# A two-layer transformer tower on one core: unread matmuls in front of TensorE's waits, attention's later stages one half step back, and three steps moved

## The reference

```python
h = tok_ffn(x[..., 0])                       # relu(x W0^T) * (x W1^T), times Wo^T
h = layernorm(h + window_attention(h))       # 16 heads of 16, |i - j| <= 64
h = layernorm(h + bitlinear_ffn(h))          # activations rounded to 8 bits, weights to -1, 0, 1
h = layernorm(h + causal_attention(h))
h = layernorm(h + moe(h))                    # 8 experts, top 2, at most 640 rows each
```

## Time and profile before

| | |
|---|---|
| time, 3 runs | 1106.05 us median, 1106.0 to 1106.23 |
| the profiled execution | 1107.4 us, its span 1105.7 us |
| PE busy | 880.9 us (80%), 4838 matmuls |
| PE weight load busy | 550.9 us (50%) |
| DVE busy | 542.7 us (49%) |
| ACT busy | 418.2 us (38%) |
| POOL busy | 297.8 us (27%) |
| mean granted TensorE clock | 0.899 of full speed |
| DMA | 81.48 MB |

### The profile page before, as it was taken

How to read it: one execution, slowest core, us unless ns; L and a number is a source line. 1 busy time by engine, 2 the same in 40 slices (tenths; PEclk the granted TensorE clock), 3 DMA queues, 4 the chain that set the end, 5 groups by cost and what they waited for, 6 DMA issues and landing times. The chain is left out here.

```text
span 1105.7 us, 14051 instructions
## 1 busy us (share of the span) xinstructions
PE 880.9 (80%) x4838; PEld 550.9 (50%) x4838; DVE 542.7 (49%) x2103; ACT 418.2 (38%) x717; POOL 297.8 (27%) x364
## 2 busy tenths in 40 slices
PE   6697889768688778888968788633999999999940
PEld 3454445534444434434524434321677787778830
DVE  1267424768668678777785777241021112111137
ACT  1325324466466476576545445300312211221002
POOL 5002312413413413212333242415021122112232
PEclk9897999979979889988988979665999999999975
DMA  9873250631532523412365420106113441343242
GB/s 355 134 179 42 30 65 15 67 37 22 61 36 35 61 24 44 54 21 27 45 90 73 56 62 21 40 24 259 56 20 115 124 128 22 113 124 66 24 100 76
DMA packets 57446, 81.48 MB, mean 74 GB/s; under 512 B 6560, under 2 KB 50977, under 8 KB 54944
## 3 DMA queue, kind: packets, MB, share of 16 engines
q1 hardware_dynamic: 49456, 70.48, 31.9%
q0 software_dynamic: 7296, 9.47, 5.1%
q10 hardware_dynamic: 624, 0.63, 0.2%
HBM read 35.37 MB, written 19.68 MB: 50 GB/s over the span
## 5 line engine op out<-in xcount | busy, mean ns | idle before, releaser
L1031 DVE CUSTOM_DVE_ANT_0 junk<-ps,maskb 128x256 bf16<-128x256 f32 (+4 forms) x512 | 205.9, 435 | 118.3 <-PE ps L755 117.1
L583 ACT ACTIVATE probs<-ps 128x512 f32<-128x512 f32 (+1 forms) x304 | 158.0, 550 | 103.0 <-PE ps L778 100.4
L1498 PE MATMUL ps<-dxT,w1s 128*128 128x320 f32 x512 | 141.9, 439 | 2.3 <-DVE dxT L1562 2.3
L1510 PE MATMUL ps<-w2s,hTe 128*128 128x256 f32 x640 | 139.3, 379 | 0.0
L1510 PEld LDWEIGHTS ps<-w2s,hTe 128*128 128x128 f32 x640 | 121.1, 190 | 16.3
L1532 ACT ACTIVATE hTe<-ps,b1s 128x640 f32<-128x640 f32 x64 | 50.8, 794 | 204.6 <-PE ps L1498 204.6
L1457 POOL DMA_INDIRECT mixed_rows<-ysb,ids x40 | 61.7, 1543 | 228.9 <-DVE ysb L1580 226.0
L755 PE MATMUL ps<-ks,qs 96*128 96x256 bf16 (+4 forms) x512 | 107.4, 294 | 19.9 <-DMA ks<-parts 8.7
L778 PE MATMUL ps<-qs,ks 99*128 99x256 bf16 (+4 forms) x512 | 107.3, 297 | 19.1 <-DMA qs<-nrows 7.9
L1498 PEld LDWEIGHTS ps<-dxT,w1s 128*128 128x128 f32 x512 | 98.5, 193 | 43.7 <-DVE dxT L1562 2.9
L794 PE MATMUL ps<-probs,vaug 128*32 128x256 f32 (+4 forms) x1024 | 94.9, 447 | 13.6 <-POOL probs L493 12.4
(11 more groups left out here) (171 smaller groups left out, 1196.3 us busy)
## 6 DMA issues: line engine op xcount, KB each, us to landing
qs<-parts SPq DMA_DIRECT2D x96, 128.0 KB, 4.9
ks<-parts SPq DMA_DIRECT2D x96, 128.0 KB, 7.5
w1s<-w SPq DMA_DIRECT2D x8, 1024.0 KB, 9.4
w2s<-w SPq DMA_DIRECT2D x8, 1024.0 KB, 4.9
dispatched_rows<-att SPq DMA_DIRECT2D x8, 650.0 KB, 16.5
dx<-dispatched_rows SPq DMA_DIRECT2D x8, 650.0 KB, 7.6
x_sb<-xT SPq DMA_DIRECT2D x8, 256.0 KB, 6.1
mixed_rows<-h SPq DMA_DIRECT2D x4, 512.0 KB, 5.6
```

What stands on the lines that cost most here:

```text
L583: act.activation(probs_of(u)[:, heads[0]:heads[-1] + 1, :], turned_bank((u, half, i))[:, 0:len(heads) * w].rearrange("p (j n) -> p j n", n=w),
L1031: ins = dve.tensor_tensor_reduce(out=junk[:, AT["s", (u, half, i)][0], a * (hi - lo):(a + 1) * (hi - lo)], in0=score_bank((u, half, i))[:, ...
L1498: ins = mm(bank(2 * (n % 2) + c)[:, 0:HC], w1s[:, e % 2, k, m * P:(m + 1) * P], dxT[:, e % 2, k, c * HC:(c + 1) * HC], start=(k == 0), sto ...
L1510: ins = mm(bank(4 + n % 2)[:, 0:D], hTe[:, e % 2, m, t * P:(t + 1) * P], w2s[:, e % 2, m, :], start=(m == 0), stop=(m == MH - 1))
```

## The change

A helper issues matmuls whose result nobody reads: `identb` (128x128) times 512 columns of `maskb`, both bf16, into the PSUM bank that is opened next and overwritten by the real work.

It is called with the bank already open and ahead of the wait: 24 times before the first scores (unit 0, whose wait for the first stack moves behind them), 12 before each of the four `fqT` turns, 3 before each of the 16 `f` turns, 10 before the turn of `gate` 3 only, 10 before each of the four counts `cnt`, 12 before `wq` 0 only, and 8 (written out) in the experts' block. Its core, with the other edits:

```diff
-TO_ROWS, TO_TURNED, TO_VALUES, TO_BACK, TO_HEADS = 10, 14, 18, 27, 28
+TO_ROWS, TO_TURNED, TO_VALUES, TO_BACK, TO_HEADS = 11, 15, 19, 28, 29
-STEPS = {... "route": 12 ...}
+STEPS = {... "route": 13 ...}
 # SP
+def load_x(b):
+    sp.wait_ge(*d_full(("tok", b - 1, f"u{ME - 1}")))
+    for k in range(KD):
+        sp.dma_start(x_sb[:, k, :], xT[0, k * P:(k + 1) * P, b * S:(b + 1) * S]).then_inc(x_in, 16)
-if phase == "tok" and c == 8 and i + 1 < B:
...
+if phase == "tok" and c == 8 and i < 2:
+    load_x(i + 1)
+if phase == "qkv" and i == 1 and c == 5:
+    load_x(3)
 if phase == "qkv":
     for j, part in STACKS[c]:
 # POOL
-if phase == "qkv" and c == 7:
+if phase == "qkv" and c in (6, 7):
...
-    for k in range(2):
+    for k in (c - 6,):
...
-if phase == "route" and c >= 8:
-    t = c - 8
+if phase == "route" and c >= 9:
+    t = c - 9
 # ACT
-if (eta - 25) % 8 == 0 and 0 <= eta - 25 < 2 * UNITS:
+if (eta - 26) % 8 == 0 and 0 <= eta - 26 < 2 * UNITS:
 # PE
 if phase == "ffn" and c == FQT:
+    o = d_open(("ffn", i, "fqT"))
+    keep_busy(o, 12)
+    o = o.bitcast(BF16)
     pe.wait_ge(fq_done, i + 1)
...
-if phase == "route" and c == 3:
+if phase == "route" and c == 5:
+    o = d_open(("route", i, "cnt"))
+    keep_busy(o, 10)
     pe.wait_ge(chosen, i + 1)
 # DVE, in route(i, c): the steps that follow the count
-if c == 5:
+if c == 6:
-if c == 6:
+if c == 7:
-if c == 7:
+if c == 8:
 # experts' block, SP
 def load_rows(e):
+    if e:
         sp.dma_start(dx[:, e % 2, :, :], dx_v[e]).then_inc(rows_in[e % 2], 16)
+    else:
+        for t in range(CT):
+            sp.dma_start(dx[:, 0, t, :], dx_v[0][:, t, :]).then_inc(first_in[t], 16)
 # experts' block, PE
 def turn_rows(e):
-    pe.wait_ge(rows_in[e % 2], 16 * (e // 2 + 1))
+    if e:
+        pe.wait_ge(rows_in[e % 2], 16 * (e // 2 + e % 2))
     for t in range(CT):
         n = e * CT + t
+        if e == 0:
+            pe.wait_ge(first_in[t], 16)
...
+pe.wait_ge(scattered, 16 * 2 * NTT)
+for _ in range(8):
+    mm(bank(0), identb[:, :], maskb[:, 0:S], start=True, stop=True)
 turn_rows(0)
```

More of the change, by code:

```diff
@@ L101 @@
     ("gate", 1, 219), ("route", 1, 221), ("o", 6, 245), ("gate", 2, 251), ("route", 2, 253), ("o", 7, 278), ("gate", 3, 284), ("route", 3, 286))
-STEPS = {"tok": 12, "qkv": 8, "o": 6, "ffn": 16, "gate": 2, "route": 12, "bias": 2, "wq": 4}
+STEPS = {"tok": 12, "qkv": 8, "o": 6, "ffn": 16, "gate": 2, "route": 13, "bias": 2, "wq": 4}
 FQT, FIRST_TILE, PER_TILE = 3, 3, 2
@@ L125, in dense_units @@
     if phase == "route":
-        return ("cnt",) if c == 3 else ()
+        return ("cnt",) if c == 5 else ()
     if phase in ("bias", "wq"):
@@ L279, in build @@
         y_out = sem("y_out")
+        first_in = [sem(f"first_in{t}") for t in range(CT)]
         xT_mm, xT_done, f1_mm, silu_done, f2_mm, y_sum, y_done, ids_done, gate_chain = (
@@ L515, in dense @@
                             pool.tensor_copy(parts[:, c - 2, 1, :], proj[:, c % 2, :]).then_inc(part1_done, 1)
-                        if phase == "qkv" and c == 7:
+                        if phase == "qkv" and c in (6, 7):
                             l, b = divmod(i, B)
-                            if i == 0:
+                            if i == 0 and c == 6:
                                 pool.wait_ge(*d_out(("bias", 1, "one")))
-                            for k in range(2):
+                            for k in (c - 6,):
                                 t = b * NT + 2 * k
@@ L709, in _ @@
                     for eta in HALVES:
-                        if (eta - 25) % 8 == 0 and 0 <= eta - 25 < 2 * UNITS:
-                            heads_out((eta - 25) // 8)
+                        if (eta - 26) % 8 == 0 and 0 <= eta - 26 < 2 * UNITS:
+                            heads_out((eta - 26) // 8)
                         e = eta - TO_ROWS
@@ L743, in t_open @@
                         return opened("t", key)
+                    def keep_busy(o, n):
+                        for _ in range(n):
+                            mm(o, identb[:, :], maskb[:, 0:S], start=True, stop=True)
                     def scores(u, half):
                         q = block_of(u)
-                        if u % 8 == 0 and half == 0:
-                            pe.wait_ge(stack_in[q % NR], STACKED * (q // NR + 1))
                         t = u % NT
@@ L752, in scores @@
                             o = s_open((u, half, i))
+                            if u == 0 and half == 0:
+                                pe.wait_ge(mask_done, 1)
+                                keep_busy(o, 24)
+                            if u % 8 == 0 and half == 0 and i == 0:
+                                pe.wait_ge(stack_in[q % NR], STACKED * (q // NR + 1))
                             for a, j in enumerate(heads):
@@ L826, in early @@
                         if phase == "ffn" and c == FQT:
+                            o = d_open(("ffn", i, "fqT"))
+                            keep_busy(o, 12)
+                            o = o.bitcast(BF16)
                             pe.wait_ge(fq_done, i + 1)
-                            o = d_open(("ffn", i, "fqT")).bitcast(BF16)
                             for n in range(2 * NT):
@@ L938, in dense @@
                             if t is not None:
+                                o = d_open(("ffn", i, f"f{t}"))
+                                keep_busy(o, 3)
+                                o = o.bitcast(BF16)
                                 pe.wait_ge(fq2_done, NT * i + t + 1)
-                                o = d_open(("ffn", i, f"f{t}")).bitcast(BF16)
                                 for k in range(MI):
@@ L946, in dense @@
                             if c == 0:
+                                if i == B - 1:
+                                    keep_busy(d_open(("gate", i, "T0")), 10)
                                 pe.wait_ge(ln_done, NORMED["o", B + i] + NT)
@@ L958, in dense @@
                                 ins.then_inc(d_full(("gate", i, "lg"))[0], 1)
-                        if phase == "route" and c == 3:
+                        if phase == "route" and c == 5:
+                            o = d_open(("route", i, "cnt"))
+                            keep_busy(o, 10)
                             pe.wait_ge(chosen, i + 1)
-                            o = d_open(("route", i, "cnt"))
                             mf = mk[:, :, :, :].rearrange("p t a b -> p (t a b)")
@@ L976, in dense @@
                                 pe.wait_ge(prep, 2)
+                            o = d_open(("wq", i, "one"))
+                            if i == 0:
+                                keep_busy(o, 12)
                             pe.wait_ge(w_sum, i + 1)
-                            mm(d_open(("wq", i, "one"))[:, 0:4], ones, wsc[:, 4 * i + 12:4 * i + 16], start=True,
+                            mm(o[:, 0:4], ones, wsc[:, 4 * i + 12:4 * i + 16], start=True,
                                stop=True).then_inc(d_full(("wq", i, "one"))[0], 1)
@@ L1276, in dense @@
                                 normed(0, NT, x, b, ROOTS["o", i])
-                        if phase == "route" and c < 8:
+                        if phase == "route" and c < 9:
                             route(i, c)
@@ L1414, in load_rows @@
                     def load_rows(e):
-                        sp.dma_start(dx[:, e % 2, :, :], dx_v[e]).then_inc(rows_in[e % 2], 16)
+                        if e:
+                            sp.dma_start(dx[:, e % 2, :, :], dx_v[e]).then_inc(rows_in[e % 2], 16)
+                        else:
+                            for t in range(CT):
+                                sp.dma_start(dx[:, 0, t, :], dx_v[0][:, t, :]).then_inc(first_in[t], 16)
                     load_w1(0)
```

## The result

The changed kernel took 1090.66 us (median of four executions: 1088.0, 1088.3, 1093.1, 1100.7), 0.986 of the time before (95% interval 0.983 to 0.989), 15.4 us less against a forecast of 21. Five more executions gave 1088.57 us and a ratio of 0.984 (0.982 to 0.987). The direction and the range held. What no part of the forecast had is the spread: the kernel before keeps within 5 us in each set of executions, the nine of the changed one cover 1080.6 to 1100.7.

A forecast was written before the change was run, and what follows sets the result against it. TensorE was taken to set the pace in most stretches, a VectorE and ScalarE chain in the ffn stretches. Terms summed to 20.8 us, taking 1107.4 to 1086.6, with the median 1.35 lower: 1085 us, range 1068 to 1100.

The forecast's parts named there:

- (1): Later attention stages one half step later: the wait for `nparts` goes, 7 us gained, 0.5 lost after the last scores.
- (2): Last x load issued ahead of the twelve stacks: its wait and the half clock behind it shrink, 5.5 us gained.
- (3): 12 products before each fqT: the wait stays, the clock behind it returns sooner, 4 us gained, bounds 0 and 10.2.
- (4): 3 products before each of 16 f tiles: mostly hidden where DVE sets the pace, 0, bounds -6.5 and +5.
- (5): Route: count matmul two half steps later with ten products, +2 us, bounds -6.5 and +8; split bias add +0.5.
- (6): 10 products before gate 3, in a 4.60 us PE wait: +0.5 us, 2.0 if the clock is held.
- (8): Experts' head: one row load per tile leaves only the last tile's part, +2.3 us; 8 products, +0.5.
- rival C: Products cover only part of waits, clock does not hold: 1091 us, 12%; sign: PE busier by 30 us, clock 0.90.
- (7): 12 products before the first wq matmul, which had no wait: -1 us, bounds -2.6 and 0; 24 at the start: 0.
- The clock: PE halves its clock behind long waits; half the work there is lost: 10.2 us at `fqb`, 16.6 ffn, 14.4 routes and scatters.
- Rival B: The clock pays in full, half the losses at fqT, f tiles and routes return: 1070 us, 12%.
- rival D: Products arrive late, in front of waits already over, and delay real work by 15.6 us: 1113 us, 5%.

The follow-up runs named there:

- e2: Changed kernel without any unread product, all moves kept (later stages, x load, route, bias add, rows in five loads): 1090.48 us, ratio 0.985.
- e6: Changed kernel without the 12 products ahead of the first weight scale (wq): 1084.52 us, ratio 0.979.
- e1: Changed kernel run again with no edit: median 1088.57 us, ratio 0.984; its profiled execution took 1080.6 us.
- e12: Changed kernel without the 12 products at wq and the 48 ahead of the f tiles: 1085.42 us, ratio 0.980.
- e7: Changed kernel keeping all moves but only the 10 products ahead of gate 3 and the 8 ahead of the experts' rows: 1089.93 us, ratio 0.984.
- the first profile: Profile of the changed kernel, unedited, from the slowest of its first four executions: 1100.7 us.
- e10: Changed kernel without any product and with the route's count at step 3 again, what follows one step earlier: 1096.0 us, ratio 0.989.
- e3: Kernel before with all 190 unread products and none of the moves: 1103.87 us, ratio 0.997.

## Why the prediction was right or wrong

The ledger in medians, from the kernel before at 1107.4 (the intervals are some 2 us to each side, so single terms below that mean little): later stages and x 11.2, the route's move 5.5, bias add and row loads 0.5, which gives e2 at 1090.5; products other than wq's 6.0 (e6, 1084.5); wq's back 4.1 (e1, 1088.6).

- **(1) and (2) together** were 7 - 0.5 + 5.5 = 12, measured 11.2. The split was wrong in kind: the later stages alone give 1.9. I had named what could take the gain (banks that VectorE frees) and not the nearest thing behind it, the wait for x, which is later in the same queue and grew by 2.2 us. The 5.6 us of (2) alone are as forecast.
- **(3) the fqT products, 4**, were tried only with those at the start and at the counts. Those three kinds bring about 4.5 us (e12 against e7). The clock behind the waits does return sooner: around these four turns e2 stands at 0.50 for 10.2 us each time, the first profile for 3.4 to 6.8, and e1 for 3.4 at the first and not at all at the others.
- **(4), 0**: right, 0.9 with intervals that overlap.
- **(5), 2 for the route's move**: under-sized, 5.5. I had taken VectorE as the bound there because it lost only 0.65 us behind the mask. The profiles of e2 and e10 say otherwise for routes 0 and 1. Half steps 176 to 224 hold route 0, and take 100.0 us in e2 against 103.3; the wait of route 1 falls just behind the scores of half step 224 (the expectations count it too early), and from there to half step 255 it is 56.6 against 60.7.
- **(6) and (8)**: 0.5 and 2.8 forecast; nothing to be told in time. The split gave 1.2 us in the first profile, since a piece of a fifth takes three quarters of the whole's landing time; the forecast had counted only the last tile's part. The fixed cost that the prediction took from the Trainium skill ("DMA: Bandwidth & Descriptors", Anatomy of one DMA) was not paid one piece after the other: the five landed within 1.6 us. That section describes transfers issued by GpSimd, and these are SyncE's. The clock did not hold at gate 3 in the first profile or in e1, as rival C had it, and no run shows it holding the experts' first matmuls at 2.4 GHz.
- **(7), -1**: measured -4.1, of which the timelines show 2.6. My step said that the wait of group 0 for `nparts`, once gone, would take most of the products' cost. It did not: that gain was there to be had without them.
- **The clock** failed as a step, not as a size. I took a saved share of half clock as a steady sum, and left what the moves do to the clock at nothing. Up to 735 us the stretches at half clock add up to 146 us in the profile before, 178 in e2's with the moves alone, 140 in the first profile after and 90 in e1's. The four ffn stretches (half steps 60 to 76, 91 to 107, 123 to 139, 155 to 171) together took 198.0, 203.7, 203.7 and 194.2 us: there the moves alone lost time, and the products gave it back in one execution and not in the other. What decides between the two stays open. The rule that I cited for rival C, from the Trainium skill ("TensorE: Matmul & The Clock Gate", Part 4: PE-mode transpose), was not tested by a run of its own.

Rival B (1070) and rival D (1113) were both wrong for the whole, but D's mechanism is real at wq, where products stood in front of a wait that did not exist. The measured 1090.7 is rival C's number, 1091, and the first profile meets the sign that the prediction gave for it: PE busier by 46 us at a clock of 0.905. In e1 it does not: 18 us at 0.937.

That the sum came near is in part luck, since its errors cancel: later stages and x 0.8 us too much, the route 3.5 too little, bias add, gate 3 and head 3.8 forecast against about 1, the products at the start, fqT, f tiles and counts 4 against about 5, wq 3.1 too small a cost. Put right, the sum is some 19, which is what e1 gave (18.9); the first four executions, at 15.4, fall short of it by the spread.

## What to carry to other kernels

Time a filler and a move apart: here the moves give 17 us, and fillers (the unread products) give 6 where they stand in real waits and take 4 where they do not; look up the wait in the timeline before placing one (wq 0 had none, wq 2 had 5.4 us, and with the fill there the median was the lowest, 1081.0 us). A gain upstream of a wait for a transfer is only kept if the transfer starts earlier too. And where waits of about 2 us remain in a busy stretch, one profile shows one of several courses of the clock: compare several executions by time and granted clock together.

## What the runs showed of the hardware that was not expected

The granted clock is not fixed by the program. Behind the same wait of 2.20 us before the same work TensorE ran at 1.2 GHz for 6.8 us in one execution of the changed kernel and stayed at 2.4 GHz in another. At gate 0, where eleven of the profiled kernels and executions wait 2.17 us, the clock was at 0.50 for 13.7 us in two of them, for 3.4 us in four, and not at all in five. What makes the difference was not tested.

The slowest and the fastest executions of the changed kernel follow the clock: 1080.6 us at 0.937, 1088.6 at 0.920, 1100.7 at 0.905. Within a few us it says little: five executions at 0.919 to 0.921 took 1088.3 to 1093.1 us. Across kernels it says little too: e2 runs 1090.5 us at 0.89, the kernel before 1107.4 at 0.895, e3 1103.9 at 0.93.
